# One-hots of four tiles by two 512-wide instructions, with four one-hot slots and four PSUM banks in layer 1 of a graph network

## The reference

```python
h = relu(layernorm(x))
# layer 0: messages from the source's row and the edge's 64 features, mean by destination
m = relu(concat([h[src], edge_attr]) @ W_msg.T + b_msg)
m = relu(m @ W_msg2.T + b_msg2)
x = x + concat([h, segment_sum(m, dst) / count(dst)]) @ W_apply.T + b_apply
h = relu(layernorm(x))
# layer 1: attention by edge weight, softmax over the edges of a destination
alpha = exp(w - segment_max(w, dst)[dst]); alpha = alpha / segment_sum(alpha, dst)[dst]
agg = unit(segment_sum(alpha[:, None] * h[src], dst))
x = x + layernorm(unit(0.5 * (h @ W_self + b_self + agg @ W_nb + b_nb))) * gamma + beta
```

## Time and profile before

| what | value |
|---|---|
| runs | 8539.82, 8536.38, 8538.44 us; median 8538.44 |
| profiled execution | 8539.41 us, span 8537.0 us |
| TensorE busy | 5259.4 us, 62% |
| weight loads busy | 4057.1 us, 48% |
| VectorE busy | 3575.8 us, 42% |
| ScalarE busy | 1110.0 us, 13% |
| GpSimd busy | 6174.3 us, 72% |
| mean granted TensorE clock | 0.711 of full speed |
| DMA | 613.4 MB, 72 GB/s |

### The profile page before, as it was taken

The page is one execution under the profiler, slowest core; times in us unless marked ns, Lnnn a source line. Parts: engine busy times, 40 slices in busy tenths (PEclk is TensorE's granted clock), DMA queues, the critical chain, the costliest instruction groups (busy, mean ns, idle before and its releaser), DMA issues.

```text
span 8537.0 us, 114672 instructions
## 1 busy us (share of the span) xinstructions
PE 5259.4 (62%) x26549; PEld 4057.1 (48%) x26549; DVE 3575.8 (42%) x13889; ACT 1110.0 (13%) x1838; POOL 6174.3 (72%) x6510
## 2 busy tenths in 40 slices
PE   4887888888878888887844444444444444444444
PEld 3555655566556665665634334333333333333333
DVE  6344444333443443443454343333333333333336
ACT  2222222222222222222210000000000000000001
POOL 2777777777777777777657777777777777777773
PEclk9988989898898989888865555555555555555555
DMA  5322222222222222233332222111111111111112
GB/s 159 96 79 77 79 75 80 78 79 79 78 78 80 79 79 80 79 87 104 84 95 66 66 65 64 54 53 53 53 53 53 53 53 53 53 53 53 53 53 71
DMA packets 393173, 613.42 MB, mean 72 GB/s; under 512 B 171379, under 2 KB 248927, under 8 KB 392223
## 3 DMA queue, kind: packets, MB, share of 16 engines
q0 software_dynamic: 206336, 422.99, 18.3%
q1 hardware_dynamic: 186784, 189.85, 8.0%
HBM read 576.45 MB, written 35.92 MB: 72 GB/s over the span
## 4 chain that ended last, share of the span: by engine, by line
POOL 61%; issue 23%; PE 8%; DMA 4%; DVE 3%; POOLq 1%; SPq 1%; DVEq 0%; ACT 0%; ACTq 0%
POOL rows_ring L449 61%; PE bank L907 3%; DMA rows_ring<-p_table,idx 2%; PE bank L969 2%; DMA idx<-in_src_ring 1%; PE bank L966 1%; PE bank L904 1%; PE bank L1031 1%; POOLq L443 0%; DVE xq L629 0%; DVE acc L629 0%; POOLq L445 0%; DVE acc L614 0%; DVE stat L597 0%; DVE acc L717 0%
## 5 line engine op out<-in xcount | busy, mean ns | idle before, releaser
L449 POOL DMA_INDIRECT rows_ring<-p_table,idx x3224 | 3070.8, 952 | 1149.0 <-issue 1094.3
L780 DVE TENSOR_TENSOR acc<-acc,bank 128x128 f32 x6448 | 1829.3, 284 | 4826.0 <-PE bank L907 4813.9
L449 POOL DMA_INDIRECT rows_ring<-h_table,idx x3224 | 3050.6, 946 | 1025.7 <-issue 982.2
L907 PE MATMUL bank<-onehot,rows_ring 128*128 128x128 f32 x6448 | 1646.5, 436 | 2322.5 <-DMA rows_ring<-h_table,idx 2322.1
L907 PEld LDWEIGHTS bank<-onehot,rows_ring 128*128 128x128 f32 x6448 | 1415.5, 323 | 2553.4 <-issue 2363.9
L783 DVE TENSOR_SCALAR onehot<-iota,dloc,coef 128x128 f32<-128x128 f32 x6448 | 2340.8, 368 | 20.7 <-ACT coef L503 18.7
L907 PEld LDWEIGHTS bank<-wmat,work 128*128 128x128 f32 x7248 | 1104.0, 219 | 48.9 <-DVE acc L848 9.4
L907 PE MATMUL bank<-wmat,work 128*128 128x128 f32 x7248 | 1100.9, 303 | 11.6 <-DVE acc L848 10.0
L969 PE MATMUL bank<-work,we_sb 64*128 64x512 f32 x1612 | 987.4, 695 | 0.0
L907 PE MATMUL bank<-onehot,work 128*128 128x128 f32 x6448 | 945.3, 295 | 3.0 <-DVE onehot L783 2.9
L966 PE MATMUL bank<-ident,rows_ring 128*128 128x128 f32 x3224 | 546.6, 295 | 628.8 <-DMA rows_ring<-p_table,idx 624.0
(11 more groups left out here) (118 smaller groups left out, 837.9 us busy)
## 6 DMA issues: line engine op xcount, KB each, us to landing
work<-in_edge_t SPq DMA_DIRECT2D x403, 256.0 KB
rows_ring<-p_table,idx POOLq DMA_INDIRECT x3224
rows_ring<-h_table,idx POOLq DMA_INDIRECT x3224, 2.5
idx<-in_src_ring SPq DMA_DIRECT2D x404, 8.0 KB, 1.6
ht_rows<-rows_ring SPq DMA_DIRECT2D x25, 256.0 KB, 2.4
p_table<-rows_ring SPq DMA_DIRECT2D x25, 256.0 KB, 2.5
work<-ht_rows SPq DMA_DIRECT2D x25, 256.0 KB, 2.6
h_table<-work SPq DMA_DIRECT2D x25, 256.0 KB, 2.3
```

The source lines that it names most:

```text
L449: pool.indirect_dma_start(out=rows_ring[:, 16 * h + G * k + j, :], out_offset=None, in_=table[:, :], in_offset=bass.IndirectOffsetOnAxis(a ...
L780: dve.tensor_tensor(win, win, ps_agg[k % 2][:, j * P:(j + 1) * P], ALU.add).then_inc(added, 1)
L907: ins = pe.matmul(tiles(dst)[t], left[t], right[t] if isinstance(right, list) else right, start=bias is None and n == 0, stop=n == len(pai ...
```

## The change

- A group's four one-hots are no longer made by four tensor_scalar instructions of 128x128 but by two tensor_tensor instructions of 128x512: a compare of `iota`, repeated for each of four tiles, with four columns of `dloc`, each repeated 128 times; and, in place, a multiplication by four columns of `coef`, repeated in the same way.
- Their place in VectorE's step changes: the compare stands behind the wait for the sums and ahead of the four additions, the multiplication behind them and behind a wait for the compare (`hot_compared`).
- In layer 1 there are four one-hot slots (two more in `work`, `place[2:4]`) and four banks for sums (the two of `ps_z` too), and VectorE adds the sums of g - 4 at the step that makes the one-hots of g. TensorE waits for the additions of g - 4 instead of g - 2. Layer 0 keeps two slots, two banks and its lag of 2.

```diff
+        ps_sum = [banks[6:8], banks[6:8] + banks[0:2]]
+        hot_slots = [[onehot[:, n, :] for n in range(2)]]
+        hot_slots.append(hot_slots[0] + place[2:4])
...
-            def sums_and_onehots(i, k, lag_sum, lag_hot, in_psum, added, hot):
+            def sums_and_onehots(layer, i, k, lag_sum, lag_hot, in_psum, added, hot):
+                slots = (2, 4)[layer]
                 adds, hots = live(i, k, lag_sum), live(i, k, lag_hot)
                 gs, gh = 8 * i + k - lag_sum, 8 * i + k - lag_hot
                 if adds:
                     at = bases(gs)
                     dve.wait_ge(in_psum, gs + 1)
-                for j in range(G):
-                    if adds:
-                        if later(gs * G + j):
-                            dve.wait_ge(added, gs * G + j)
-                        win = acc[:, ds(at[j], P)]
-                        dve.tensor_tensor(win, win, ps_agg[k % 2][:, j * P:(j + 1) * P], ALU.add).then_inc(added, 1)
-                    if hots:
-                        t = gh * G + j
-                        ins = dve.tensor_scalar(onehot[:, k % 2, j * P:(j + 1) * P], iota[:, :], dloc[:, ds(t, 1)], coef[:, ds(t, 1)],
-                                                ALU.is_equal, ALU.mult)
                 if hots:
-                    ins.then_inc(hot, 1)
+                    hot4 = four(hot_slots[layer][k % slots])
+                    dloc4, coef4 = (arr[:, ds(gh * G, G)].unsqueeze(2).to_broadcast([P, G, P]) for arr in (dloc, coef))
+                    dve.tensor_tensor(hot4, iota[:, :].unsqueeze(1).to_broadcast([P, G, P]), dloc4, ALU.is_equal).then_inc(S["hot_compared"], 1)
+                for j in range(G) if adds else ():
+                    if later(gs * G + j):
+                        dve.wait_ge(added, gs * G + j)
+                    win = acc[:, ds(at[j], P)]
+                    dve.tensor_tensor(win, win, ps_sum[layer][k % slots][:, j * P:(j + 1) * P], ALU.add).then_inc(added, 1)
+                if hots:
+                    dve.wait_ge(S["hot_compared"], layer * NG + gh + 1)
+                    dve.sem_inc(S["vector_turns"], 1)
+                    dve.tensor_tensor(hot4, hot4, coef4, ALU.mult).then_inc(hot, 1)
...
-                    sums_and_onehots(i, k, 2, 0, S["sums1_in_psum"], S["sums1_added"], S["onehot1_ready"])
+                    sums_and_onehots(1, i, k, 4, 0, S["sums1_in_psum"], S["sums1_added"], S["onehot1_ready"])
...
-                        g, slot = 8 * i + k, k % 2
+                        g, slot = 8 * i + k, k % 4
                         pe.wait_ge(s_rows[1][k], 64 * i + 64)
                         pe.wait_ge(S["onehot1_ready"], g + 1)
-                        if later(g, 2):
-                            pe.wait_ge(S["sums1_added"], 4 * g - 4)
-                        products(ps_agg[slot][:, :], [([rows_ring[:, G * k + j, :] for j in range(G)], tiles(onehot[:, slot, :]))]).then_inc(S["sums1_in_psum"], 1)
+                        if later(g, 4):
+                            pe.wait_ge(S["sums1_added"], 4 * g - 12)
+                        products(ps_sum[1][slot][:, :], [([rows_ring[:, G * k + j, :] for j in range(G)], tiles(hot_slots[1][slot]))]).then_inc(S["sums1_in_psum"], 1)
```

More of the change, by code:

```diff
@@ L166, in gnn @@
             scalars_staged scalars_turned coef_filled sums_zeroed0 dloc_ready x_reloaded
-            counts_made m1t_in_psum m1t_ready m2_in_psum m2_ready onehot0_ready sums0_in_psum sums0_added
+            counts_made m1t_in_psum m1t_ready m2_in_psum m2_ready hot_compared onehot0_ready sums0_in_psum sums0_added
             x1_sums_copied x1_in_psum x1_added var1_ready root1_ready normed1_ready h2_ready sums_zeroed1
@@ L774, in sums_and_onehots @@
                     dve.wait_ge(in_psum, gs + 1)
-                for j in range(G):
-                    if adds:
-                        if later(gs * G + j):
-                            dve.wait_ge(added, gs * G + j)
-                        win = acc[:, ds(at[j], P)]
-                        dve.tensor_tensor(win, win, ps_agg[k % 2][:, j * P:(j + 1) * P], ALU.add).then_inc(added, 1)
-                    if hots:
-                        t = gh * G + j
-                        ins = dve.tensor_scalar(onehot[:, k % 2, j * P:(j + 1) * P], iota[:, :], dloc[:, ds(t, 1)], coef[:, ds(t, 1)],
-                                                ALU.is_equal, ALU.mult)
-                if hots:
-                    ins.then_inc(hot, 1)
+                if hots:
+                    hot4 = four(hot_slots[layer][k % slots])
[10 more added lines that the diff above has]
+                    dve.tensor_tensor(hot4, hot4, coef4, ALU.mult).then_inc(hot, 1)
             def layer0(i):
                 for k in range(8):
-                    sums_and_onehots(i, k, 2, 0, S["sums0_in_psum"], S["sums0_added"], S["onehot0_ready"])
+                    sums_and_onehots(0, i, k, 2, 0, S["sums0_in_psum"], S["sums0_added"], S["onehot0_ready"])
             dve.wait_ge(S["coef_filled"], FILLS)
```

## The result

The changed kernel takes 8972.75 us (four runs, 8969.03 to 8974.65) beside 8538.97 us of the kernel before: a ratio of 1.0508, 95% interval 1.0495 to 1.0521. It is slower by 434 us. The forecast was 9190 with a range of 8940 to 9380; the direction and the place hold, the size was put too high by half.

A forecast was written before the change was run, and what follows sets the result against it. GpSimd's gathers were taken to bound both layers, so VectorE matters only where it delays a gather. The terms summed as 8539 - 15 + 362 + 10 + 295 = 9191, say 9190 us, range 8940 to 9380.

The forecast's parts named there:

- rival D: Weak hold in both layers: only 0.53 us holds, or phases drift; 0.16 us less per hit, 8950 us; chance 0.06.
- C: Compare starts 0.22 us or more later, misses in layer 1, multiply hits instead: 227 for 362, 9055 us; chance 0.06.
- (1): One-hots in both layers: the small gather delays of the narrow ones mostly go, -15 us.
- (2): Compare in layer 1: starts median 0.10 us ahead of a gather and delays it, 0.46 us a group, 362 us.
- (3): Multiply behind the additions in layer 1: free if the compare hit, holds a later gather if it missed, 10 us.
- rival B: Double hit: multiply starts over 0.13 us earlier and holds a gather too, about 9660 to 9800 us; chance 0.08.
- (4): Layer 0: starts spread more, so compare and multiply both hold gathers; taken as 295 us.
- (5): VectorE's step grows from 1.9 to 2.8 or 3.0 us, covered by the lag of both layers: costs 0.
- (6): Four slots and banks in layer 1: TensorE waits there for landed rows, not one-hots or banks; worth 0.

The follow-up runs named there:

- psum_inputs_b: Changed kernel's wide one-hots with two slots, two banks, lag two in layer 1, one input of each in PSUM, and a further wait: 8525.1 us.
- reordered_b: Changed kernel with VectorE's step reordered: addition, compare, two additions, multiply, addition, both SBUF inputs kept: 8617.8 us, ratio 1.0088 to the kernel before.
- slots_only_b: Kernel before with only the four one-hot slots, four banks and lag four in layer 1, narrow one-hots kept: 8542.6 us beside 8545.1.
- hots_only_b: Changed kernel's wide one-hots in both layers, but two slots, two banks and lag two in layer 1: 8936.5 us beside 8545.1.
- extra_896: Kernel before plus one 896-wide tensor_tensor with two SBUF inputs per group of layer 1, first behind the wait for the sums: 9092.4 us.

## Why the prediction was right, and where its sizes were off

Direction and mechanism were right: gathers bound both layers, and the second SBUF input holds them. With one input in PSUM, 1560 wide instructions of the same length that begin in the zone of the holds hold no gather (psum_inputs_b), and a change of place alone, both inputs kept, took five sixths of the slowdown away (reordered_b).

That the time lies inside the range is in part luck. By the prediction's own account the main case reached from 8985 to 9375 us, and 8973 is below that; the range went down to 8940 only for rival D, a hold that covers 0.53 of the 0.69 us, and for C. D isn't what happened: a compare that hits costs all of itself that lies beyond 0.12 us behind the gather's start (0.51 us for the one of 6203.24). It is the zone of starts that is narrower, which happens to be by the same 0.16 us. Layer 1 came out at 287 us, at the low end of its 280 to 450; layer 0 at 155, below its 180 to 400.

Step by step:

(1) The wide form takes 0.69 us, as read from the earlier trace rows, and the 15 us of the narrow one-hots came out: psum_inputs_b is 19 us under the kernel before, with an interval of 12 to 30.

(2) The compare in layer 1 was put at 362 us. In the changed kernel compares hold gathers for 235 us. The term is too large because of the edge of the zone. The rows gave the point of 0.12 us after the gather's start at which its hold begins to count, and I took it for the last start that still holds too, since among the rows of two-input instructions there was no start between 0.08 us ahead and 0.29 us behind. The edge lies 0.04 to 0.05 us ahead. In the changed kernel 177 of 803 compares start between it and +0.12, where the prediction had them at the full price. By the starts of before, the edge alone takes the 362 down to 306. The compare also starts 0.02 us later behind its wait than an addition does. Rival C, which let a late start lose the hold, needed 0.22 us more; with the median start at 0.10 us ahead, 0.06 puts half of the compares past the edge.

(3) The multiply's place was right (2.07 to 2.29 us behind the compare predicted, 2.16 measured), and it hardly meets the gather behind a held one, as rival B had it: 27 of 803 multiplies start 0.05 to 0.25 us ahead of any gather. But "the phase stays what it is" holds only while the compare hits. A compare that misses leaves the multiply 0.32 us ahead of a gather, that hold moves the following gathers but not the next compare, and the next compare hits early in its zone, for 0.28. Two groups then pay 0.54 together instead of 0.46 to 0.51 each. The multiply's share of layer 1 is 52 us against 10 predicted.

(4) Layer 0 was put at 295 and came out at 155. Zones of 0.53 us instead of 0.69 are most of it: with the measured edge, the starts of before give 62 us for the compare and 161 for the multiply. The rest went as gathers shifted: the holds of the changed kernel add up to 67 and 92 us. How the starts settle there, beside TensorE's own waits, I haven't taken apart.

(5) and (6) hold. TensorE waits for one-hots for 4.4 us in all in layer 0 (the row of bank<-onehot,work in the page above), and slots and banks cost nothing beside narrow one-hots (slots_only_b); beside wide ones up to the 36 us of hots_only_b stay open.

On the two statements of the Trainium skill (SBUF — State Buffer, "Who interferes with whom"): that an instruction with two SBUF inputs contends with a GpSimd instruction that reads SBUF is what these gathers show. That tensor_tensor doesn't stall a DMA issued by GpSimd doesn't hold here for a gather: extra_896, a plain tensor_tensor, holds it for up to 0.92 us. The same page, section "SBUF: two separate sides", gives the port to whichever starts first, for its whole instruction, while the other stands. Where VectorE comes first, the traces above agree. Where the gather does, they don't: the compare of 6310.73 stood for 0.05 us and not for the gather's 0.94, and the compare of reordered_b at 6201.37, 0.20 us into a gather, took its plain 0.68.

## What to carry to other kernels

Where GpSimd's gathers set the pace, look at what VectorE runs as each of them starts, not at how long VectorE is busy: an instruction with two SBUF inputs that begins ahead of a gather adds what is left of it, and one a tenth of a microsecond later adds nothing. Reading one input from PSUM removes the hold altogether, and fewer, wider instructions make it longer if one does hit. Since both loops are tied to each other, nearly the same distance between them comes back in every group, and a tenth of a microsecond in a start can be worth 200 us at the end.

## What the runs showed of the hardware that was not expected

- The order is decided 0.04 to 0.05 us ahead of a gather's recorded start, to about 0.01 us, while the hold counts from 0.12 us after it. A compare that came just too late stood until 0.03 us behind the gather's start: up to 0.76 instead of 0.69 us.
- Where a second wait, long satisfied, stands behind the one that VectorE is held up by, the compare starts 0.07 us later: 0.24 us behind the products' end in the three kernels that have it, 0.16 in the two that lack it.
- A compare that reads a PSUM bank and writes one takes 0.70 us at 128x512, as from SBUF to SBUF (0.69).
- One chip runs the kernel before in 11232 instead of 8540 us, with pauses on several engines; there hots_only is 2% faster than the kernel before (0.9789) in spite of the holds. What makes the pauses, and why wide one-hots help there, stays open.
